# Expert routing by scattered token rows and accumulated output rows, in place of gathered rows and reloaded pairs

## The reference

```python
x = x + gnn(layernorm(x), src, dst, ...)      # edge sums, three small layers with relu, residual
xn = layernorm(layernorm(x)) * gamma + beta
logits = xn @ Wr + br
top_vals, top_idx = top_k(logits, 2);  w = softmax(top_vals)
for e in range(8):                            # W1[e]: 256 x 512, W2[e]: 512 x 256, all fp32
    h = gelu(xn @ W1[e] + b1[e], approximate=False)
    y = y + (h @ W2[e] + b2[e]) * w_full[..., e, None]
x = x + y
```

## Time and profile before

| | us |
|---|---|
| median of 3 runs (lowest, highest) | 471.32 (471.03, 485.67) |
| span of the profiled execution | 472.4 |
| TensorE busy, 4,344 products | 380.4 (81%) |
| VectorE busy | 294.7 (62%) |
| ScalarE busy | 222.6 (47%) |
| GpSimd busy | 135.4 (29%) |

### The profile page before, as it was taken

How to read it: one execution, slowest core, us unless ns; L and a number is a source line. 1 busy time by engine, 2 the same in 40 slices (tenths; PEclk the granted TensorE clock), 3 DMA queues, 4 the chain that set the end, 5 groups by cost and what they waited for, 6 DMA issues and landing times.

```text
span 472.4 us, 12881 instructions
## 1 busy us (share of the span) xinstructions
PE 380.4 (81%) x4344; PEld 346.1 (73%) x4345; DVE 294.7 (62%) x704; ACT 222.6 (47%) x351; POOL 135.4 (29%) x241
## 2 busy tenths in 40 slices
PE   0895598999998889980449999999999999999200
PEld 0684498999998667770349999999999999999100
DVE  2886998999994753568945444445444444444853
ACT  2475576888885274560025444444444444443000
POOL 3050000000000500000054665665666665653200
PEclk9987589999999977875559999999999999999755
DMA  9620299999999269930011222212222222215899
GB/s 202 154 54 3 40 183 199 214 220 222 216 222 200 63 241 362 375 116 0 0 58 58 77 70 72 72 67 67 75 69 73 72 67 67 75 60 135 207 228 310
DMA packets 112696, 62.15 MB, mean 132 GB/s; under 512 B 86625, under 2 KB 106743, under 8 KB 112544
## 3 DMA queue, kind: packets, MB, share of 16 engines
q1 hardware_dynamic: 101168, 41.80, 36.6%
q0 software_dynamic: 6272, 14.93, 10.2%
q10 hardware_dynamic: 5232, 5.12, 3.7%
HBM read 27.70 MB, written 13.64 MB: 88 GB/s over the span
## 4 chain that ended last, share of the span: by engine, by line
PE 70%; DMA 9%; DVE 8%; ACT 5%; issue 4%; SPq 3%; POOL 0%; ACTq 0%; DVEq 0%; POOLq 0%
PE psum L918 20%; PE psum L929 19%; PE psum L790 9%; PE psum L781 7%; DMA w_sb<-pair_rows 3%; PE psum L837 3%; PE psum L859 3%; PE psum L907 2%; DMA at<-cts 2%; DMA b_rows<-in_L_ffn_b_dram 2%; PE psum L721 1%; DMA pair_rows<-yb,scol 1%; SPq L288 1%; PE psum L712 1%; ACT cts L591 1%
## 5 line engine op out<-in xcount | busy, mean ns | idle before, releaser
L918 PE MATMUL psum<-xgT,w_now 128*128 128x128 f32 x832 | 103.2, 278 | 0.0
L918 PEld LDWEIGHTS psum<-xgT,w_now 128*128 128x128 f32 x832 | 98.8, 195 | 0.2 <-issue 0.2
L929 PE MATMUL psum<-w_sb,hT 128*128 x416 | 98.4, 380 | 0.0
L591 ACT CAST cts<-psum 128x1000 bf16<-128x1000 f32 x100 | 78.4, 815 | 23.7 <-PE psum L781 23.3
L929 PEld LDWEIGHTS psum<-w_sb,hT 128*128 128x128 f32 x416 | 75.1, 190 | 8.3 <-issue 0.3
L679 ACT ACTIVATE hT<-up 128x512 f32<-128x512 f32 x52 | 32.8, 630 | 97.7 <-DVE up L1347 97.7
L790 PE MATMUL psum<-z,at 125*128 (+1 forms) x1875 | 71.0, 195 | 3.2 <-DMA at<-cts 3.2
L668 ACT COPY w_now<-w_sb 128x1024 f32 x52 | 54.4, 1046 | 34.5 <-DVEq L1312 21.9
L790 PEld LDWEIGHTS psum<-z,at 125*128 125x128 bf16 x1875 | 65.9, 100 | 3.8 <-DMA at<-cts 2.1
L1347 DVE TENSOR_TENSOR up<-psum,b1T 128x512 f32<-128x512 f32 x52 | 36.0, 692 | 47.8 <-PE psum L918 47.8
L492 POOL DMA_INDIRECT pair_rows<-yb,scol x52 | 52.0, 999 | 46.9 <-issue 33.6
(11 more groups left out here) (228 smaller groups left out, 347.8 us busy)
## 6 DMA issues: line engine op xcount, KB each, us to landing
w_sb<-in_L_ffn_W_dram SPq DMA_DIRECT2D x2, 4096.0 KB, 20.4
token_rows<-tok SPq DMA_DIRECT2D x5, 560.0 KB
tok<-pair_rows SPq DMA_DIRECT2D x5, 560.0 KB
w_sb<-pair_rows SPq DMA_DIRECT2D x5, 560.0 KB
out_dram<-res ACTq DMA_DIRECT2D x5, 560.0 KB
res<-in_x_dram ACTq DMA_DIRECT2D x3, 560.0 KB
res<-in_x_dram SPq DMA_DIRECT2D x2, 560.0 KB
b_sb<-in_L_ffn_b_dram SPq DMA_DIRECT2D x1, 1024.0 KB, 23.8
```

Source lines behind the costliest of these rows:

```text
L591: act.copy(cts[:, par, :, d0:d0 + nw * WD].rearrange("p h (b d) -> p b h d", b=nb), psum[:, bank:bank + nb, 0:wb * WC].rearrange("p b (d h ...
L918: last = pe.matmul(psum[:, j % 2, c * P:(c + 1) * P], w1_now[:, j % 2, k, c * P:(c + 1) * P], xgT[:, j % 2, k, :], start=(k == 0), stop=(k ...
L929: last = pe.matmul(psum[:, 4 + j % 2, 0:D], hT[:, j % 2, k, :], w2_sb[:, ds(e, 1), k, :].rearrange("p a h -> p (a h)"), start=(k == 0), st ...
```

## The change

Ranking goes group by group inside the token stage, and data moves by position instead of by gathered index.

- Each expert owns a fixed region of 26 x 128 rows in a DRAM tensor `slot_rows` (1,088 bytes a row: the token, 8 gate arguments, its output row number). For each group VectorE chooses the experts (`choose`), TensorE ranks the group's tokens on top of the groups before (`rank`), VectorE makes the positions (`place`), and GpSimd scatters every tile twice (`scatter_tokens`), 50 scatters in all.
- A block is then a plain load of 128 rows by SyncE (`load_block`). The first 12 blocks (`EARLY`) are full blocks of the first two groups (`FIRST_GROUPS`); VectorE computes the rest of the block lists between the first blocks' steps (`early_needs`, `later_rows`, `pads_where`, `later_needs`).
- GpSimd copies gate arguments and row numbers out of the loaded rows (`take`). ScalarE makes the gate, a sigmoid by way of Tanh, and multiplies the block's rows by it (`gate_rows`). GpSimd adds the weighted rows into the output by an accumulating indirect DMA (`add_rows`). The output is first set to `res` by SyncE.
- Two adds may not meet on one output row, so `need_i` says, for each block and each of four landing semaphores, what must have landed before.
- Unused rows in an expert's last block get a gate of zero and a distinct row number. The pair rows, index lists, one-hot arithmetic, reload, weighting and final store go.

The core of the diff (order of GpSimd's queue whole; removed lines and VectorE's index arithmetic left out):

```diff
+EARLY = 12
+FIRST_GROUPS = 2
 # SyncE
-            sp.wait_ge(got_key, (n_rounds + 1) * 16 * NG)
...
+                sp.wait_ge(h3_used, (g + 1) * len(H3))
+                spread(sp, out_t[:, g * G:(g + 1) * G, :], res[:, g * G:(g + 1) * G, :], out_init)
+            def load_block(b, j, i, last=False):
+                row = sp.value_load(row_i[0:1, ds(b, 1)], min_val=0, max_val=SLOTS - P)
+                if not (static(b) and b < 4):
+                    sp.wait_ge(xgT_psum, b - 3)
+                    sp.nop(nofuse=True)
+                    sp.wait_ge(xg_taken, 2 * (b - 3))
+                    sp.nop(nofuse=True)
+                sp.dma_start(xg[:, j, :], slot_dram[ds(row, P), :]).then_inc(xg_in[j], 16)
...
+            sp.wait_ge(blocks_ready, 1)
+            sp.wait_ge(tok_scattered[0], 16 * 2 * G * FIRST_GROUPS)
+            for b in range(EARLY):
+                load_block(b, b % 4, b // 4)
 # GpSimd
+            def scatter_tokens(g):
+                pool.wait_ge(tok_norm, (g + 1) * G)
+                pool.wait_ge(pos_ready, g + 1)
...
+                for t in range(g * G, (g + 1) * G):
+                    for k in range(2):
+                        pool.indirect_dma_start(out=slot_dram,
+                                                out_offset=bass.IndirectOffsetOnAxis(ap=pos_i[:, k, t:t + 1], axis=0),
+                                                in_=tok[:, t, :], in_offset=None
+                                                ).then_inc(tok_scattered[0 if g < FIRST_GROUPS else 1], 16)
+            def take(b, j, i):
+                n = slot_of(b, j)
+                pool.wait_ge(xg_in[j], 16 * (i + 1))
+                if not static(b):
+                    pool.nop(nofuse=True)
+                    pool.wait_ge(down_sb, b - 3)
+                    pool.nop(nofuse=True)
+                    pool.wait_ge(scattered[j], 16 * i + BASE)
+                pool.nop(nofuse=True)
+                pool.tensor_copy(tagged[:, n, :], xg[:, j, D:ID]).then_inc(xg_taken, 1)
+                pool.tensor_copy(scol[:, n:n + 1], xg[:, j, ID:ID + 1]).then_inc(xg_taken, 1)
+            def add_rows(b, j, i):
+                n = slot_of(b, j)
+                if not (static(b) and b < 1):
+                    for s_ in range(4):
+                        landed = pool.value_load(need_i[0:1, ds(4 * b + s_, 1)], min_val=BASE, max_val=16 * (NB // 4) + BASE)
+                        pool.wait_ge(scattered[s_], landed)
+                        pool.nop(nofuse=True)
+                pool.wait_ge(xg_taken, 2 * (b + 1))
+                pool.wait_ge(down_sb, b + 1)
...
+                pool.indirect_dma_start(out=out, out_offset=bass.IndirectOffsetOnAxis(ap=scol[:, n:n + 1], axis=0),
+                                        in_=yb[:, n, :], in_offset=None, compute_op=ALU.add).then_inc(scattered[j], 16)
+            for g in range(3):
+                scatter_tokens(g)
+            for b in range(0, 4):
+                take(b, b % 4, b // 4)
+            scatter_tokens(3)
+            for b in range(4, 8):
+                take(b, b % 4, b // 4)
+            scatter_tokens(4)
+            for b in range(8, EARLY):
+                take(b, b % 4, b // 4)
+            pool.wait_ge(out_init, 32 * NG)
...
+            pool.wait_ge(needs_ready, 1)
+            for b in range(EARLY):
+                add_rows(b, b % 4, b // 4)
 
             def block(b, j, i, last):
-                    gather_column(b + 4, j)
-                    gather_block(b + 4, j)
-                    scatter_block(b - 2, (j - 2) % 4)
+                if not (last and j == 3):
+                    take(b + 1, (j + 1) % 4, i if j < 3 else i + 1)
+                add_rows(b, j, i)
+            take(EARLY, 0, EARLY // 4)
...
+            later_blocks(pool, last_q, block)
 # ScalarE, after gelu of block b, for block b - 1
+            def gate_rows(b, j, i):
+                n = slot_of(b, j)
+                e = act.value_load(ebi[0:1, ds(b, 1)], min_val=0, max_val=NX - 1)
+                act.wait_ge(xg_taken, 2 * (b + 1))
+                act.activation(gate[:, j % 2, 0:1], tagged[:, n, ds(e, 1)], ACT.Tanh, scale=0.5).then_inc(gate_th, 1)
...
+                act.activation(gate[:, j % 2, 1:2], gate[:, j % 2, 0:1], ACT.Identity, bias=half_col[:], scale=0.5).then_inc(gate_sb, 1)
...
+                act.wait_ge(down_raw, b + 1)
+                if not (static(b) and b < EARLY):
+                    act.wait_ge(scattered[j], 16 * i + BASE)
+                act.activation(yb[:, n, :], yraw[:, j % 2, :], ACT.Copy, scale=gate[:, j % 2, 1:2]).then_inc(down_sb, 1)
 # TensorE
+            def rank(g):
+                pe.wait_ge(chosen_sb, g + 1)
+                pe.matmul(psum[0:T, 3, RANK:RANK + G * NX], later[0:T, 0:T], sel[:, grp, :].rearrange("p t e -> p (t e)"),
+                          start=True, stop=True, skip_group_check=True)
+                for t in range(G - 1):
...
+                last.then_inc(rank_psum, 1)
...
                 if k < NG:
                     third_layer(k)
+                if 0 <= k - 2 < NG - 1:
+                    rank(k - 2)
+            for b in range(EARLY):
+                expert_step(b, b % 4, b // 4, False)
+                if b == 0:
+                    rank(NG - 1)
 # VectorE
             for k in range(NG + 1):
                 if k >= 1:
                     scales2(k - 1)
+                if k >= 2:
+                    choose(k - 2)
+                    place(k - 2)
+                if k - 2 == FIRST_GROUPS - 1:
+                    early_blocks()
                 if k < NG:
                     residual_group(k)
                     moments2(k)
```

More of the change, by code:

```diff
@@ new lines, in build @@
+        scol = sb("scol", [P, EARLY + 3], I32, lt)
+        gate = sb("gate", [P, 2, 2], F32, lt)
+        pos_i = sb("pos_i", [T, 2, NT], I32, lt)
+        mask = sb("mask", [T, 2, G, NX], F32, lt)
+        sel = sb("sel", [T, NT, NX], BF16, lt)
+        base16 = sb("base16", [T, NG + 1, NX], BF16, lt)
+        logit = sb("logit", [T, G, NX], F32, lt)
+        rt = [sb(f"rt{i}", [T, G, NX], F32, lt) for i in range(3)]
+        top = sb("top", [T, 5, G], F32, lt)
+        slot_pos = sb("slot_pos", [T, G, NX], F32, lt)
@@ L521, in _ @@
+            pool.nop(nofuse=True)
+            pool.wait_ge(got_key, (n_rounds + 1) * 16 * NG)
         @block.scalar
@@ new lines, in place @@
+            def place(g):
+                to = slot_pos0 if g == 0 else slot_pos
+                dve.wait_ge(rank_psum, g + 1)
+                done(dve.tensor_tensor(to[:], psum[0:T, 3, RANK:RANK + G * NX].rearrange("p (t e) -> p t e", e=NX),
+                                       first_row[0:T], ALU.add))
+                if g in (FIRST_GROUPS - 1, NG - 1):
+                    done(dve.tensor_copy(nex[:, 0, :], psum[:, 3, COUNT:COUNT + NX]))
+                settle()
+                done(dve.tensor_tensor(picked[:], mask[:], to[:].unsqueeze(1).broadcast_to([T, 2, G, NX]), ALU.mult))
+                settle()
+                with nc.allow_low_precision("whole numbers below 2**24"):
+                    done(dve.tensor_reduce(pos_i[:, :, g * G:(g + 1) * G], picked[:], AX.X, ALU.add))
+                settle()
+                dve.engine_nop().then_inc(pos_ready, 1)
@@ new lines, in early_blocks @@
+            def early_blocks():
+                floor_of(nex[0:1, 1, :], nex[0:1, 0, :], 0.5, 1.0 / P)
+                done(dve.tensor_tensor_scan(nex[0:1, 2, :], ones[0:1, 0:NX], nex[0:1, 1, :], 0.0, ALU.mult, ALU.add))
+                done(dve.tensor_scalar(nex[0:1, 3, :], nex[0:1, 1, :], -float(P), float(REGION * P), ALU.mult, ALU.add))
+                settle()
+                gates_of(past[:, 0:EARLY, :], nex[0:1, 2, :], EARLY)
+                with nc.allow_low_precision("whole numbers of at most 8"):
+                    done(dve.tensor_reduce(ebi[:, 0:EARLY], past[:, 0:EARLY, :], AX.X, ALU.add))
+                total(col[:, 0, 0:EARLY], nex[0:1, 3, :], EARLY)
+                done(dve.tensor_tensor(row_i[:, 0:EARLY], col[:, 0, 0:EARLY], blk_row[:, 0:EARLY], ALU.add))
+                settle()
+                dve.engine_nop().then_inc(blocks_ready, 1)
```

592 lines of the change are left out of this document (298 added, 294 removed).

## The result

The changed kernel takes 524.35 us (median of 4 runs, 518.45 to 529.27) against 477.19 beside it: a ratio of 1.1035, 95% interval 1.0899 to 1.1171. The forecast was 510, from 444 to 548, with 0.70 on slower. Ratios compare only executions that the chip did not disturb (a run with too few of them has no ratio), and the profiled one of the changed kernel (span 525.5, clock 0.879) is itself a disturbed one. Positions are therefore also counted from the end of the edge part.

The account below looks back on a forecast made before the run. TensorE bounded the old blocks; GpSimd's queue would decide now: adds start at 264 us, plus 38 and waits of 10 give 312, add 12 at 316, 39 x 4.3 + 21 gives 505, landing and closing 510; range 444 to 548.

Parts of the forecast that it names:

- Scatters of 1.52 us: GpSimd's token scatters over 125 partitions: 1.52 us each, 50 of them 76 us.
- The queue runs dry nowhere: GpSimd during the token scatters: later positions come well before their turn, so scatters end at 260 us.
- An early add 3.42: GpSimd's adds up to block 11: four register loads of 0.67 plus 0.74, 3.42 us each.
- A later one 4.3: GpSimd's add with its take, after block 12: four loads of 0.80 plus 0.74 and 0.33, rounded to 4.3 us.
- Landing 4.2: GpSimd's accumulating DMA into the output: a read of 2.8 plus a scatter of 2.4 less 1.0, 4.2 us.
- landing waits of 10 and 21: GpSimd's waits at ends of experts: 5 early of 2.0 us make 10, 15 later of 1.4 make 21.
- Closing 5: After the last add: its landing of 4.2 us and about 1 for closing.
- TensorE starts at the last logits' end, near 225: TensorE's expert blocks: held only behind the last logits in its queue, so starting 18 us earlier than before.
- TensorE standing 30 us near block 12: TensorE wants block 12 near 283 us, but its gate waits for a take behind add 11 at 312.
- (a): Expert blocks: TensorE stays the bound, a register load costs GpSimd only 0.17 us; 446 us, chance 0.17.
- (b): GpSimd's adds land like a plain scatter, 2.4 us, mostly hidden: 477 us, no change; chance 0.13 with other low-end meetings.
- (c): ScalarE's gates: Tanh and Gelu pull different tables, two loads of 1.28 us a block; 511 us, chance 0.03.

Follow-up runs that it names:

- the private rows: Changed kernel with one register load per add, each block added into output rows of its own and all landing counts zero: 452.30 us, ratio 0.9510.
- constants: Changed kernel with GpSimd's part written out for these inputs, same waits against fixed numbers, no register loads or loop branches: 475.74 us, ratio 0.9821.

## Why the prediction was right

**The mechanism.** GpSimd's queue, with its scatters, then four loads and their waits per add, sets the end: 15 us put on it come out as 8.9; loads cut to one turn the ratio of 1.10 into 0.98, waits taken away turn 524 us into 480; both taken away give TensorE its bound back. Loads and waits are not separate bills. Cutting loads saves 53.3 us with waits and 301.0 - 275.8 = 25.2 without; dropping waits saves 47.3 with four loads, 19.2 with one. The total is 72.5 either way. (From the first add to the last alone these are 49.4, 26.5, 43.4 and 20.5.) With both gone TensorE's pace caps the gain. A slow cycle leaves no slack in which a wait could lie.

**Terms of the sum, by the forecast's own steps.**
- Scatters of 1.52 us: 1.49, right. "The queue runs dry nowhere" was wrong: the rows scattered for the first two groups, the last issued at 221.2, were back in SBUF for the first take only at 241.6, and GpSimd stood 5.58 us for them (0 to 3.3 in the other profiles).
- An early add 3.42: 2.97 (0.60 a load, not 0.67). A later one 4.3: 3.82, or 4.01 with the loop's branch (0.69 a load, not 0.80). Too dear by 11 x 3.42 - 33.6 = 4.0 and 39 x 4.3 - 156.3 = 11.4 us.
- Landing 4.2: 3.8. Yet landing waits of 10 and 21: 12.9 and 30.7. I had let the loads of the next add hide more of a landing than they do. The errors cancelled against the cycle's, and that is luck: 48 + 4 + 189 = 241 forecast, 46.5 + 4.9 + 187.0 = 238.4 measured.
- Closing 5: 8.7. No row of the views covers the 5 us from the last landing (516.82 + 3.8) to the end.
- TensorE starts at the last logits' end, near 225: wrong, harmlessly. They ended at 230.3 (219.8 without the edge part's shift), but the first up product came at 243.30 (232.8), 13.0 behind: block 0's rows had to be scattered, landed and loaded first. That is 10.7 us ahead of the 243.55 of the earlier trace rows, where the forecast had 18. The last group's ranking did run beside the first blocks, as forecast, but only because it too had to wait: VectorE's queue holds it behind block 0's first step. TensorE's timeline, and VectorE's where that ranking begins:

```profile
241.65 1.08 PE L1011 MATMUL psum<-ident,xg 128*128 128x128 f32 x4 [11.39 <-DMA xg<-slot_rows]
```

```profile
243.07 0.19 DVE L1289 TENSOR_TENSOR logit<-psum,br_bet 125x40 f32<-125x40 f32 x1
```

The forecast held TensorE back only by its queue, and forgot that the gap it saw closing was now the rows' own way through DRAM.
- TensorE standing 30 us near block 12: the place right, the size too large. ScalarE's timeline and, below it, TensorE's:

```profile
326.89 0.20 ACT L746 ACTIVATE gate<-tagged 128x1 f32 x1 [15.16 <-POOL tagged L544]
```

```profile
329.49 0.69 PE L1011 MATMUL psum<-ident,xg 128*128 128x128 f32 x2 [12.02 <-DMA xg<-slot_rows]
```

The gate of block 12 waited 15.16 us for its take, and TensorE 12.02 behind it; with 6.16 before the up products at 311.26 it stood some 18.
- Not in the sum at all: the edge part, "not touched by the change", 10.5 us longer in this execution, 5.1 of it by the tiles' place. Its first transpose starts 5.3 later besides (60.5 and 55.2); four variants' profiles have that start at 54.5 to 55.1, so this half comes and goes and isn't the change's.

**The rivals.** (a) TensorE the bound at 446 is what came once loads and waits were both gone: a profiled 449.5. The cover that I denied is there in part: where I saw no engine work to hide loads under, the first of an add's four starts 0.22 us ahead of the DMA instruction of the add before it, and the next two start within its 1.56. So four loads lengthen an early cycle from 1.86 to 2.97, 0.28 a load: nearer to this rival's 0.17 than to 0.67. The forecast's 3.42 came out because it let that instruction lie under the loads in turn. (b) A landing like the plain scatter's is refuted by the least of 52 landings, 3.6. By the same token the Trainium skill, "DMA: Bandwidth & Descriptors" (Anatomy of one DMA), whose terms gave an estimate of 2.3, doesn't agree with this trace for an accumulating DMA. (c) Table loads: ScalarE's timeline holds one between the token stage and the first blocks and none at the gates:

```profile
233.53 1.28 ACT L763 ACT_TABLE_LOAD   x1
249.03 0.63 ACT L763 ACTIVATE hT<-up 128x512 f32<-128x512 f32 x1 [14.22 <-DVE up L1482]
...
252.11 0.63 ACT L763 ACTIVATE hT<-up 128x512 f32<-128x512 f32 x1 [1.39 <-DVE up L1482]
252.76 0.20 ACT L746 ACTIVATE gate<-tagged 128x1 f32 x1
```

Tanh follows gelu at once, so the lists of "ScalarE: Activation LUTs" (Table sets) in the Trainium skill, which don't show them together, say nothing against it here.

**What stays open.** Why the address of the edge part's tiles matters, and which of them it is, was not tried. Nor was a way to keep the landing waits off (adds into two outputs, say), which the private rows price at 19 us.

## What to carry to other kernels

An engine that looks idle in the busy shares can be the bound by its queue: count every register load and wait between two of its instructions, see which of them can run while the engine still has work, compare the cycle with the bound engine's, and remember that a cycle above it leaves no slack to hide a wait in. Read a number once and derive the rest in registers. An accumulation into shared rows brings an order, and each boundary of that order costs a landing; and a change that shifts tile addresses can move code that it doesn't touch, so read the untouched stage after as well.

## What the runs showed of the hardware

- A register load from SBUF holds GpSimd's queue for 0.60 us (fixed address) to 0.69 us (computed), wait included; register arithmetic in place of three loads costs next to nothing (early adds 1.86 us apart, as with constants). Loads can run ahead, beside work that the engine still has: then adds with four loads each came 1.93 and 1.89 apart.
- An accumulating indirect DMA of 128 rows of 1 KB: 1.56 us of GpSimd, 3.6 to 4.4 to land, against 0.99 and 2.4 for the same scatter without accumulation.
- The take's two copies last 0.77 us each beside an add in the loop and 0.19 alone.
- 50 DMA transposes go 2.07 to 2.14 us apart or 1.97 by whether the edge part's tiles start 64 bytes further in SBUF.
